# GpSimd's xb add moved to the front of its step in a two-layer hypergraph block

## The reference, cut to what matters

```python
def hypergraph_conv(x, adj, W, b):
    H = (adj != 0).astype(x.dtype)
    w = adj.reshape(N, -1)[:, :C]
    xw = jnp.einsum('ncd,hd->nch', x, W)
    Dn = 1 / einsum('nce,ne->nc', H, w)        # 0 where the sum is 0
    Be = 1 / H.sum(axis=1)                     # 0 where the sum is 0
    m = Be[:, :, None] * jnp.einsum('nce,nch->neh', H, xw)
    return Dn[:, :, None] * jnp.einsum('nce,neh->nch', H, m) + b

h = relu(hypergraph_conv(x, adj, W1, b1))      # 256 -> 512
h = layer_norm(h, gamma, beta)
y = hypergraph_conv(h, adj, W2, b2)            # 512 -> 256
out = _layernorm(x + (y + x), axis=-1)
```

## Time and profile before

| | us |
|---|---|
| median of 3 runs | 315.39 (314.51 to 316.2) |
| the profiled execution | 318.37 |
| its span, first to last instruction | 316.6 |
| TensorE busy | 291.8 (92%) |
| VectorE busy | 237.2 (75%) |
| ScalarE busy | 218.1 (69%) |
| GpSimd busy | 132.1 (42%) |
| mean granted TensorE clock | 0.97 |

### The profile page before, as it was taken

The page is one execution under the profiler, slowest core; times in us unless marked ns, Lnnn a source line. Parts: engine busy times, 40 slices in busy tenths (PEclk is TensorE's granted clock), DMA queues, the critical chain, the costliest instruction groups (busy, mean ns, idle before and its releaser), DMA issues.

```text
span 316.6 us, 5880 instructions
## 1 busy us (share of the span) xinstructions
PE 291.8 (92%) x1918; PEld 261.4 (83%) x1918; DVE 237.2 (75%) x581; ACT 218.1 (69%) x627; POOL 132.1 (42%) x162
## 2 busy tenths in 40 slices
PE   7677999999999999999999999999999999899381
PEld 6656989899898989898988989898989889797270
DVE  0295559787878889697878787897969787879416
ACT  4469666879687887878796868878787767465400
POOL 2213062635436180917263452708081635444501
PEclk9799899999999999999999999999999999999776
DMA  7911121040412223130404031111212030101011
GB/s 223 294 37 34 34 71 30 10 157 4 131 35 80 88 69 99 66 102 18 151 0 143 24 100 36 66 68 66 69 67 69 5 128 2 66 2 51 18 65 66
DMA packets 26437, 22.55 MB, mean 71 GB/s; under 512 B 860, under 2 KB 26152, under 8 KB 26408
## 3 DMA queue, kind: packets, MB, share of 16 engines
q1 hardware_dynamic: 26304, 22.15, 22.0%
q10 hardware_dynamic: 104, 0.04, 0.0%
HBM read 13.80 MB, written 8.39 MB: 70 GB/s over the span
## 4 chain that ended last, share of the span: by engine, by line
DVE 44%; POOL 27%; issue 12%; PE 8%; ACT 3%; DMA 3%; SPq 1%; DVEq 0%; POOLq 0%
POOL xb_sb L772 11%; POOL rstd L765 7%; DVE g_sb L592 6%; DVE bn_sb L629 6%; DVE pair_sb L607 6%; DVE z_sb L621 6%; DVE r_lo L601 6%; DVE u_lo L564 5%; POOL r_hi L780 5%; POOL rstd L787 5%; DVE q_sb L612 3%; DMA w_raw<-in_L_gnn_W_dram 3%; DVE mv_sb L639 2%; PE bank_v L247 1%; PE bank_g L270 1%
## 5 line engine op out<-in xcount | busy, mean ns | idle before, releaser
L601 DVE TENSOR_TENSOR r_lo<-r_sb,r_hi 128x512 fp32r<-128x512 f32 x64 | 75.6, 1200 | 31.6 <-POOL r_hi L780 31.4
L270 PE MATMUL bank_g<-w_hi,r_hi 128*128 128x258 f32 x256 | 70.6, 307 | 0.0
L787 POOL TENSOR_TENSOR rstd<-var,half_power 128x4 f32<-128x4 f32 (+1 forms) x17 | 17.6, 1037 | 125.5 <-DVE var L643 125.5
L272 PE MATMUL bank_g<-w_lo,r_hi 128*128 128x256 f32 x256 | 65.0, 285 | 0.0
L442 ACT ACTIVATE r_sb<-bank_v,vec 128x512 f32<-128x512 f32 x64 | 44.2, 691 | 24.9 <-PE bank_v L262 24.1
L780 POOL TENSOR_SCALAR r_hi<-r_sb 128x512 fp32r<-128x512 f32 x64 | 46.6, 728 | 25.7 <-ACT r_sb L442 25.6
L262 PE MATMUL bank_v<-u_hi,w_hi 128*128 128x512 f32 x128 | 52.0, 406 | 0.7 <-DVE u_lo L564 0.7
L262 PE MATMUL bank_v<-u_lo,w_hi 128*128 128x512 f32 x128 | 50.6, 395 | 0.0
L262 PE MATMUL bank_v<-u_hi,w_lo 128*128 128x512 f32 x128 | 50.5, 395 | 0.0
L270 PEld LDWEIGHTS bank_g<-w_hi,r_hi 128*128 128x128 f32 x256 | 49.4, 193 | 1.3
L272 PEld LDWEIGHTS bank_g<-w_lo,r_hi 128*128 128x128 f32 x256 | 49.1, 192 | 1.3
(11 more groups left out here) (93 smaller groups left out, 480.6 us busy)
## 6 DMA issues: line engine op xcount, KB each, us to landing
x_sb<-in_x_dram SPq DMA_DIRECT2D x16, 512.0 KB, 3.5
out_dram<-z_sb SPq DMA_DIRECT2D x15, 512.0 KB, 3.0
adj_sb<-in_adj_dram SPq DMA_DIRECT2D x16, 256.0 KB, 4.1
w_raw<-in_L_gnn_W_dram SPq DMA_DIRECT2D x2, 512.0 KB, 6.2
out_dram<-z_sb SPq DMA_DIRECT2D x2, 256.0 KB, 2.2
b_half<-in_L_gnn_b_dram SPq DMA_DIRECT2D x1, 128.0 KB, 7.9
edge_rows<-in_adj_dram ACTq DMA_DIRECT2D x1, 32.0 KB, 3.2
vec_rows<-in_L_gnn_b_dram ACTq DMA_DIRECT2D x1, 2.0 KB
```

The costliest lines, as they stand in the source:

```text
L270: pe.matmul(bank_g[:, n, 0:W2COLS], r_hi[:, i % 2, k, graph(n)], w2_hi[:, k], start=(k == 0), stop=False)
L272: pe.matmul(bank_g[:, n, 0:DOUT], r_hi[:, i % 2, k, graph(n)], w2_lo[:, k], start=False, stop=False, skip_group_check=True)
L601: nc.vector.tensor_tensor(r_lo[:, i % 2, k], r_sb[:, k], r_hi[:, i % 2, k].bitcast(F32), ALU.subtract).then_inc(r_lo_ready, 1)
```

## The change

In GpSimd's list xb of group i goes to the front of step i, behind copy_w and a new wait for q_ready of group i. Everything else keeps its order; add_b2 itself is unchanged, its own two waits (x landed, the buffer of xb free) included.

```diff
             for i in range(G):
                 if i + 4 < G:
                     copy_w(i + 4)
+                pool.wait_ge(q_ready, i + 1)
+                add_b2(i)
                 if i:
                     inverse_std2(i - 1)
                 if i < LAST:
                     split_r(i + 1, 0)
-                add_b2(i)
                 if i == LAST:
                     break
                 split_r(i + 1, 1)
```

## The result

The changed kernel takes 307.59 us (median of 4 runs, 305.05 to 311.76), the kernel before 315.79 beside it. The ratio is 0.9705, 95% interval 0.9621 to 0.9789: faster by 3.0%, 8.2 us in the medians and 9.3 us by the ratio (0.0295 x 315.79). The forecast was 306.0 with a range of 302.8 to 309.5. The profiled execution took 309.23 us against 318.37 (9.1 less; 309.0 was forecast), with a span of 307.4 instead of 316.6.

What follows compares the result with a forecast made beforehand. TensorE was taken to bound a middle step, within 0.34 us. Gains of 4.7 (middle), 3.25 (end) and 1.5 (clock) made 9.4 us, taking the 315.39 us median to 306.0, range 302.8 to 309.5.

Steps and rivals of the forecast that it cites:

- Added wait: GpSimd's new wait for the squares in each step: costs nothing, covered by 8.29 us of idle time.
- xb in its place: GpSimd, middle step: xb starts about 0.1 us behind the squares and ends 0.85 us before rstd2 is due.
- What runs beside it: VectorE's two u_lo and bn_stats beside xb: taken as not held, cost nothing; upper bound 0.9 us a step.
- the slower rival: VectorE behind the squares: xb holds bn_stats, costing 0.9 us in 14 steps, total 318.5 us; chance 0.06.
- Statistics and g_sb: Middle steps: layer norm 1 power 0.38 us earlier, 1.11 behind the v chunks; make_y's 0.34 us wait for g_sb goes.
- Sum of the middle: Steps 1 to 12 gain 4.1 us, step 13 0.6, step 14 nothing: 4.7 us, bounds 3 and 7.
- The end: Step 15: xb starts right behind the squares, so TensorE's stand in front of L388 shrinks by 3.25 us.
- The clock: End of the kernel: shorter TensorE idling keeps the clock from falling to half; gain 1.5 us, bounds 0 and 2.05.
- The total: Whole kernel: 9.4 us gained, profiled execution 318.37 to 309.0 us, median 315.39 to 306.0.
- The chain's claim: Rival for every step: each loses xb's whole 2.40 us, 33.6 us in 14 steps, total 282; chance 0.01.

Runs made afterwards that it cites:

- e5: Changed kernel, but xb of groups 0 to 14 also waits for the second u_lo behind the squares: 307.01 us, ratio 0.967 to the kernel before.
- e4: Changed kernel, but groups 0 to 14 without xb's wait for the squares: 313.25 us, ratio 0.9899 to the kernel before.
- e1: The changed kernel run again, nothing altered: 307.07 us, ratio 0.9704 to the kernel before.
- e2: Kernel before with only the last group's xb (group 15) moved behind its squares: 312.52 us, ratio 0.9866.
- e8: Changed kernel with L388 put behind the last two g groups on TensorE: 304.86 us, ratio 0.9609 to the kernel before.
- e9: e8 with both last-group layer norm 1 powers ahead of group 14's, and both variances ahead of the g scalings: 304.13 us, ratio 0.9585.
- e10: e8 with only the last group's first layer norm 1 power put ahead of group 14's power on GpSimd: 303.87 us, ratio 0.9595.
- e7: Kernel before with L388 put behind the last two g groups on TensorE: 311.73 us, ratio 0.9821.

## Why the prediction was right

- *Added wait free.* Right: GpSimd idles 4.24 us for the squares, nothing behind it is due. e5 shows that even 1.2 us of lateness costs TensorE nothing up to step 11 and 0.2 us in each of steps 12 to 14. e4 adds what the wait is worth, which the prediction did not ask: 5.3 us.
- *xb in its place.* Right to 0.01 us in each margin (0.09 behind the squares, 0.86 ahead of the power).
- *What runs beside it.* The value taken, nothing, was right for u_lo and bn_stats, and with it the slower rival fell. The rule of the Trainium skill (SBUF — State Buffer, section "SBUF: two separate sides") was the better guide than the row of r_lo taken for all: in this trace u_lo and bn_stats, with at most one SBUF input, were not held. The prediction missed that the small mean (L642, one input, SBUF to SBUF) is of the held kind; it took 0.63 us in the last step and 1.39 in e5. By that rule it would have to run in a 2-port mode; no run shows its mode. The variance behind it and the power wait for it, but TensorE does not.
- *Statistics and g_sb.* Right: power 147.43 - 146.31 = 1.12 us behind the v chunks (1.11 forecast), make_s to g 2.43, make_y never waits in steps 1 to 12.
- *Sum of the middle.* 4.7 forecast, 5.4 measured: 4.3 for steps 1 to 12 (4.1 said), 0.56 for step 13 (0.6), 0.57 for step 14, which was counted at nothing.
- *The end.* 3.25 forecast for the stand in front of L388, 3.31 measured. Missed: TensorE now reaches the turn of squares before the squares are done, and waits 0.64 us instead of 0.24 for them; 0.4 us of step 14's gain is given back there. (The upper end of the range counts the end with 3.0 instead of 3.25; no row gives the 3.0.)
- *The clock.* The term that was mis-sized: 1.5 forecast, some 0.6 measured. The argument was that 1.88 us of standing still is shorter than the 2.6 us after which the clock had fallen. It fell all the same, at about 291.1, 1.4 us after TensorE stopped, and L388 ran at half clock; only the g behind it got the clock back. In e1, e2 and e5, which stand still for the same 1.82 us, L388 took 3.14, 3.20 and 3.03 us as well. In e4 it took 2.32: the clock was still full while TensorE stood still, and fell when TensorE had been at work again for 0.9 us, as two windows of e4 show:
```profile
295.10:295.90 0.80, 0.80 (x4) 0.72 (x5) 0.54 (x4) 0.00 (x0) 0.77 (x1) 1.00 0.00 0
296.10:297.30 1.20, 1.20 (x4) 0.94 (x3) 0.11 (x1) 0.83 (x2) 0.90 (x3) 0.50 0.00 0
```
So the step that failed is the reading of the 2.6 us of one trace as a delay that a shorter stand stays under. When exactly the clock falls varies by execution, and why stays open. In e8, where g follows the squares at once, it stayed full through g and L388 and fell only in the last make_y; in e9 and e10 it stayed full to the end of TensorE's work.
- *The total.* It is closer than its terms, and that part is luck: 0.7 more in the middle and 0.2 from the spread of the start stand against 0.3 less in front of L388 and 0.9 less from the clock, 9.1 measured (9.2 of the span) for 9.4 forecast.
- *The chain's claim*, 2.40 us in each step, was 7 times too high per step: TensorE had only 0.34 us to give.

## What to carry to other kernels

A wait's price is not the length of the instruction waited for, but what the busiest engine loses by it: compare a middle step with one that is free of the wait (here step 0). When an instruction of GpSimd is moved, look at which VectorE instructions it will stand beside, and sort them by their SBUF inputs: r_lo and, in e4, the adds of squares (two SBUF inputs) were held until it ended, and so was the small mean; u_lo (one input in PSUM) and bn_stats were not. Where two such instructions race, fix the order with a wait: an unrelated copy may be deciding it, and may be missing in the last steps.

## What the runs showed of the hardware

- An instruction of 4 elements can be held as long as a large one: mean L642, 0.17 us alone, 1.39 beside xb (e5).
- The holding goes both ways: GpSimd's r_hi of 128x512 took 1.07 us where it started beside r_lo and 0.62 in the changed kernel, where r_lo does not run beside it, and in e4 xb took 2.84 instead of 2.40 where r_lo had started first.
- The clock fell when TensorE had stood still for 1.4 us here, 2.6 us before; in e4 it fell 0.9 us after the end of a stand of 1.82 us.
- The record of the clock does not explain every duration: from 8 to 12 us it reads 1.00 in the changed kernel and in e1, yet the same make_s (L224 at 8.10) took 2.09 us in the one and 1.16 in the other.
- Executions with the same instructions up to the first make_y reach it between 45.06 (e7) and 49.08 us (e2), more than the gain of the middle's first ten steps (3.4). A single profile's span is no measure of a change of this size; the time from a common instruction on agreed to 0.1 us between the two traces of the changed kernel (259.0 and 259.1).
